# Tile 5's h and half of tile 7's normalised x: transposed by DMA instead of by TensorE

## The reference, cut to what matters

```
def fake_quant(x, s, z): q = clip(round(x / s + z), 0, 255); return (q - z) * s
x = x + tanh(g_xattn) * matmul(fake_quant(layernorm(x)), fake_quant(ctx))      # ctx: (2, 2048, 2048)
W = U * S[None, :] @ V.T                                                      # rank 512
x = x + tanh(g_ffn) * einsum('bti,oi->bto', layernorm(x), W)
```

## Time and profile before

| what | value |
|---|---|
| median of 3 runs | 588.23 us |
| the profiled execution's own time | 588.18 us |
| its span | 586.4 us |
| TensorE (PE) busy | 568.3 us, 97% |
| VectorE (DVE) busy | 447.8 us, 76% |
| ScalarE (ACT) busy | 236.0 us, 40% |
| GpSimd (POOL) busy | 196.3 us, 33% |
| chain that ended last | 94% PE, 2% DMA, 1% POOL |

### The profile page before, as it was taken

The page is one execution under the profiler, slowest core; times in us unless marked ns, Lnnn a source line. Parts: engine busy times, 40 slices in busy tenths (PEclk is TensorE's granted clock), DMA queues, the critical chain, the costliest instruction groups (busy, mean ns, idle before and its releaser), DMA issues.

```text
span 586.4 us, 7496 instructions
## 1 busy us (share of the span) xinstructions
PE 568.3 (97%) x2688; PEld 259.5 (44%) x2688; DVE 447.8 (76%) x797; ACT 236.0 (40%) x268; POOL 196.3 (33%) x146
## 2 busy tenths in 40 slices
PE   1899999999999999999999999999999999999998
PEld 0344444444444444444444444444444444444444
DVE  6959999997178982679978799798597986888222
ACT  4799888822123423648713612102530135103200
POOL 2989850000406127847541720220044005310000
PEclk9999999999999999999999999999999999999999
DMA  8999995638927796789975262423854086403722
GB/s 275 387 386 387 337 268 130 127 102 172 272 66 216 175 247 188 210 232 386 268 166 156 57 138 57 125 74 64 224 108 135 9 176 165 125 1 69 165 55 107
DMA packets 145941, 102.73 MB, mean 175 GB/s; under 512 B 108785, under 2 KB 109041, under 8 KB 145905
## 3 DMA queue, kind: packets, MB, share of 16 engines
q1 hardware_dynamic: 136912, 84.96, 55.0%
q10 hardware_dynamic: 8992, 17.30, 9.0%
HBM read 58.99 MB, written 16.78 MB: 129 GB/s over the span
## 4 chain that ended last, share of the span: by engine, by line
PE 94%; DMA 2%; POOL 1%; SPq 1%; issue 1%; DVE 0%; DVEq 0%
PE bank L616 23%; PE bank L692 19%; PE bank L661 12%; PE bank L697 9%; PE bank L755 9%; PE bank L760 9%; PE bank L756 9%; PE bank L579 2%; DMA v_hl<-in_ctx_dram 2%; SPq L331 1%; POOL u8r L270 1%; POOL q L279 1%; PE bank L711 0%; PE bank L592 0%; SPq L341 0%
## 5 line engine op out<-in xcount | busy, mean ns | idle before, releaser
L285 POOL TENSOR_SCALAR ring<-ring,bvec 128x2048 f32<-128x2048 f32 x16 | 33.4, 2089 | 259.2 <-DVE bvec L1245 259.2
L616 PE MATMUL bank<-q,qT 128*128 128x512 f16 x512 | 117.8, 381 | 0.0
L692 PE MATMUL bank<-v_hl,xT 128*128 128x512 f16 x448 | 101.3, 379 | 0.0
L290 POOL TENSOR_TENSOR ring<-ring,corr 128x512 f32<-128x512 f32 x64 | 88.9, 1419 | 22.6 <-ACT corr L967 21.6
L755 PE MATMUL bank<-u_hl,hbuf 128*128 128x512 f16 x208 | 78.9, 379 | 0.0
L756 PE MATMUL bank<-u_hl,hbuf 128*128 128x512 f16 x208 | 78.8, 379 | 0.0
L279 POOL TENSOR_SCALAR q<-u8r,const 128x1024 f16<-128x1024 uint8 x52 | 66.8, 1295 | 33.6 <-ACT u8r L864 29.8
L616 PEld LDWEIGHTS bank<-q,qT 128*128 128x128 f16 x512 | 50.3, 98 | 61.4 <-issue 1.7
L692 PEld LDWEIGHTS bank<-v_hl,xT 128*128 128x128 f16 x448 | 43.8, 98 | 52.2
L915 ACT ACTIVATE ln<-ln,const 128x1 f32<-128x1 f32 x16 | 4.7, 295 | 144.0 <-DVE ln L1342 144.0
L1416 DVE SCALAR_TENSOR_TENSOR ring<-bank,cy,ring 128x512 f32<-128x512 f32 x63 | 46.2, 745 | 17.4 <-PE bank L760 17.3
(11 more groups left out here) (173 smaller groups left out, 782.4 us busy)
## 6 DMA issues: line engine op xcount, KB each, us to landing
out_dram<-ring SPq DMA_DIRECT2D x63, 256.0 KB, 3.4
ring<-in_x_dram SPq DMA_DIRECT2D x62, 256.0 KB, 4.3
v_hl<-in_ctx_dram SPq DMA_DIRECT2D x26, 512.0 KB, 11.5
stage<-in_ctx_dram ACTq DMA_DIRECT2D x17, 512.0 KB, 5.9
u_hl<-in_L_ffn_V_dram SPq DMA_DIRECT2D x8, 512.0 KB, 11.4
corr<-in_ctx_dram ACTq DMA_DIRECT2D x8, 512.0 KB, 6.7
stage<-in_ctx_dram SPq DMA_DIRECT2D x6, 512.0 KB, 11.4
q<-in_ctx_dram ACTq DMA_DIRECT2D x4, 512.0 KB, 9.9
```

Source lines behind the costliest of these rows:

```text
L290: nc.gpsimd.tensor_tensor(xq(t, n), xq(t, n), corr[:, n * W:(n + 1) * W], ALU.add).then_inc(x1_pre, 1)
L616: mm = nc.tensor.matmul(unit_bank(t, n)[:, :], qT_of(t)[:, k, :], q2[:, n, k, :], start=(k == 0), stop=(k == KT - 1))
L692: nc.tensor.matmul(h_bank(u)[:, :], x_home(u, g)[:, half, k % 8, :], v_hl[:, k, 0, :], start=(g == 0 and a == 0 and half == 0), stop=False)
```

## The change

`H_PE`, `X_PE` and `h_pieces`, `hT_copy` are gone. Tile 5's h goes by DMA into its place in `qT` (that of the quantised row of tile 6), as soon as tile 6's stage 1 is done. Half 0 of tile 7's x goes by DMA into the place of tile 7's quantised row, once tile 7's stage 1 is done. Half 1 is still transposed by TensorE, in one call ahead of `mm4(5)`, and copied by VectorE into `xT`. All waits on counts are renumbered to fit. The diff, cut to its core:

```
-        AFTER = (TB + 1,) + tuple(second_of)
-        x_home = lambda u, g: xT[:, 0 if u in AFTER else g, :, :, :] if u not in AFTER or g else \
+        AFTER = (TB - 1, TB + 1) + tuple(second_of)
+        x_dma = lambda u, g: u + 1 - (g == 1 and u >= TB - 1)
+        x_home = lambda u, g: xT[:, 0 if u in AFTER and u > TB else g, :, :, :] if u not in AFTER or g else \
             qT_of(u).rearrange("p (a k) w -> p a k w", a=2)
...
-                elif u in h_home:
-                    sp.wait_ge(s1_done, S1_END(u))
+                elif u == TB - 3:
+                    sp.wait_ge(s1_done, S1_END(u + 1))
...
             x_transpose(6)
-            for n in range(NQ):
-                store(4, n)
-            for n in range(NQ):
-                load_x(8, n)
+            h_transpose(5)
+            store(4, 0)
+            store(4, 1)
+            x_transpose_half(7, 0)
+            store(4, 2)
+            store(4, 3)
+            load_x(8, 0)
...
-            h_pieces(5)
             mm3(6)
-            x_pieces(0)
+            x_pieces()
             mm4(5)
-            x_pieces(1)
             mm3(7)
...
-            hT_copy(5)
             x_hi_half(7, 1)
...
-            xT_copy(0)
+            xT_copy()
...
-            xT_copy(1)
             quantise(8)
```

More of the change, by code:

```diff
@@ L29, in gated_block_program @@
     NST = 10
-    H_PE = (5,)
-    X_PE = TB - 1
     NU8 = 8
@@ L124, in gated_block_program @@
         xT_in = [sem(f"xT_in{g}") for g in range(2)]
-        hT_in = sem("hT_in")
-        hT_written = sem("hT_written")
-        hT_copied = sem("hT_copied")
         xT_written = sem("xT_written")
         xT_copied = sem("xT_copied")
+        hT_in = sem("hT_in")
         y_stored = [[sem(f"y_stored{i}_{n}") for n in range(NQ)] for i in range(R)]
@@ L200, in gated_block_program @@
         h_bank = lambda u: bank[3 + u % 2]
-        x_dma = lambda u: u + 1 - (u > X_PE)
-        x_bank = lambda g, half: bank[(2 * g + half) % 3]
-        h_dma = lambda u: u + 1 - sum(v <= u for v in H_PE)
         y_bank = lambda i: bank[5 + i % 3]
@@ L367, in x_transpose_half @@
                     sp.wait_ge(mm3_half, 2 * (u - 1) + 1)
+                elif u - 1 in AFTER and u > TB:
+                    sp.wait_ge(mm3_half, 2 * u)
                 elif u >= 1:
@@ L493, in _ @@
             x_transpose(6)
-            for n in range(NQ):
-                store(4, n)
-            for n in range(NQ):
-                load_x(8, n)
+            h_transpose(5)
[5 more added lines that the diff above has]
+            load_x(8, 0)
+            load_x(8, 1)
+            load_x(8, 2)
+            load_x(8, 3)
             h_transpose(6)
@@ L586, in colsum_of_sums @@
                 if n < 2:
-                    pe.wait_ge(xT_copied, 4)
+                    pe.wait_ge(xT_copied, 2)
                 else:
@@ L678, in mm3 @@
                     pe.wait_ge(h_lo, u - 1)
-                if u - 2 in H_PE:
-                    pe.wait_ge(hT_copied, H_PE.index(u - 2) + 1)
                 if u == TB:
@@ L683, in mm3 @@
                 for g in range(2):
-                    if u == X_PE:
-                        pe.wait_ge(xT_copied, 2 * g + 2)
+                    if u == TB - 1 and g == 1:
+                        pe.wait_ge(xT_copied, 2)
                     else:
-                        pe.wait_ge(xT_in[g], 16 * x_dma(u))
+                        pe.wait_ge(xT_in[g], 16 * x_dma(u, g))
                     for a, k in enumerate(KORD[g]):
@@ L699, in mm3, with x_pieces @@
                     mm.then_inc(mm3_half, 1)
-            def x_pieces(g):
-                pe.wait_ge(xs_hi, 2 * X_PE + g + 1)
-                pe.wait_ge(xs_lo, 2 * X_PE + g + 1)
-                for half in range(2):
[L705 to L709, removed]
+            def x_pieces():
+                u = TB - 1
+                pe.wait_ge(xs_hi, 2 * u + 2)
+                pe.wait_ge(xs_lo, 2 * u + 2)
+                pe.wait_ge(x1_ready, S1_END(u))
+                for half in range(2):
+                    dst = bank[half][:, :].bitcast(f16)
                     for k in range(8):
-                        mm = nc.tensor.transpose(dst[:, k * P:(k + 1) * P], xs[:, g, half, k * P:(k + 1) * P], ident[:, :])
+                        mm = nc.tensor.transpose(dst[:, k * P:(k + 1) * P], xs[:, 1, half, k * P:(k + 1) * P], ident[:, :])
                     mm.then_inc(xT_written, 1)
[L714 to L722, removed]
             def mm4(u, n0=0, n1=NQ):
[L725 to L728, removed]
+                pe.wait_ge(hT_in, 16 * (u + 1))
                 for n in range(n0, n1):
@@ L926, in x_hi_half @@
                     act.wait_ge(p_done, 2 * NP * (first_of[u] + 1))
-                if u - 1 == X_PE:
-                    act.wait_ge(xT_written, 2 * g + 2)
+                if u == TB and g == 1:
+                    act.wait_ge(xT_written, 2)
                 elif u > 0:
-                    act.wait_ge(xT_in[g], 16 * x_dma(u - 1))
+                    act.wait_ge(xT_in[g], 16 * x_dma(u - 1, g))
                 nc.scalar.activation(xs[:, g, 0, :], xhalf(u, g), ACT.Identity, bias=bias, scale=scale).then_inc(xs_hi, 1)
@@ L941, in hid_hi @@
                 act.wait_ge(mm3_half, 2 * u + 2)
[L942 to L945, removed]
+                if u > 0:
+                    act.wait_ge(hT_in, 16 * u)
                 else:
@@ L949, in hid_hi @@
                     .then_inc(h_hi, 1)
[L951 to L955, removed]
             def column_correction(b, n):
@@ L1302, in t4 @@
                             for g in range(2):
-                                dve.wait_ge(xT_in[g], 16 * x_dma(PAIRS[p][0] - 1))
+                                dve.wait_ge(xT_in[g], 16 * x_dma(PAIRS[p][0] - 1, g))
                         else:
@@ L1376, in x_lo, with xT_copy @@
                 x_lo_half(u, 1)
-            def xT_copy(g):
+            def xT_copy():
                 for half in range(2):
[L1380 to L1383, removed]
+                    dve.wait_ge(xT_written, half + 1)
+                    dve.wait_ge(mm3_half, 2 * (TB - 2) + 2)
+                    nc.vector.tensor_copy(x_home(TB - 1, 1)[:, half, :, :].rearrange("p k w -> p (k w)"),
+                                          bank[half][:, :].bitcast(f16)).then_inc(xT_copied, 1)
             def hid_lo(u):
@@ L1396, in k_sum @@
                 elif i == 1:
-                    dve.wait_ge(xT_written, 2 + 2 * (n // 3))
+                    if n == 3:
+                        dve.wait_ge(xT_written, 2)
+                    else:
+                        dve.wait_ge(xT_in[0], 16 * TB)
                 else:
```

## The result

The changed kernel takes 592.68 us (median of 6 runs, 591.74 to 593.96) against 588.32 us (587.89 to 588.61) for the kernel before: a ratio of 1.0074, 95% interval 1.0064 to 1.0085. The forecast was 586.9 us. The 24 pieces are gone, and 4.4 us came in.

A forecast was written before the change was run, and what follows sets the result against it. TensorE, busy 568.3 of 586.4 us, was taken to bound the kernel. Own time 588.18 less 1.34 us of pieces gives 586.84; the median stands 0.05 above, so 586.9 us, all other terms nothing; range 586.4 to 588.3.

The forecast's parts named there:

- What TensorE loses, 1.34 us: TensorE's list drops 8 pieces of h (0.45 us) and 16 pieces of x (0.89 us), 1.34 us together.
- the whole gain reaches the end: After 341.26 us VectorE is pulled forward too, so all 1.34 us shorten the kernel's end.
- Tile 5's h: Its DMA fits SP's idle time, lands by 261.8 us, 9.6 us before mm4(5) wants it, and costs nothing.
- The slack of tile 7's transpose, 10.7 us: Half 0 of tile 7's x lands by 266.6 to 271.3 us, mm3(7) wants it at 281.97: no cost.
- The load on the DMA engines: Both transposes occupy the engines 4.2 us, 2.3 us fit before 260 us, so ScalarE's context loads slip 1.9 us (0 to 4.2).
- The place where a slip bites: TensorE would stall at mm4(6)'s fourth unit, through tile 6's y unit, only from a slip of 2.9 us.
- The slower rival: Loads and transposes hinder one another, slip passes 4.2 us; at 5.5 us TensorE waits 2.6 us: 589.5 us, chance 0.09.
- The rule of one set of 16 engines: DMAs of all issuers interleave on the same 16 engines, so the slip reaches ScalarE's loads despite their own queue.

The follow-up runs named there:

- the last version: Changed kernel with tile 7's transpose issued earlier, five ScalarE loads held until it landed, tile 6's upper half and tile 8's quantising ahead of chunks: 587.08 us, ratio 0.9976.
- the run with x alone: Changed kernel with tile 5's h back on TensorE and ScalarE, only half 0 of tile 7's x going by DMA: 592.26 us, ratio 1.0063.
- the extra transpose: Kernel before with all its TensorE pieces, plus one unused DMA transpose of half 0 of tile 7's x on SP: 591.36 us, ratio 1.0049.
- SP's order altered: Changed kernel with tile 7's transpose issued ahead of tile 4's stores on SP, ScalarE's loads not held: 591.02 us, ratio 1.0043.

## Why the prediction was wrong

- *What TensorE loses, 1.34 us:* right. In the last version mm3(7) starts at 282.02, 1.29 us ahead of the earlier trace rows, and 1.2 us reach the end, so "the whole gain reaches the end" held too.
- *Tile 5's h:* right. It went into SP's idle time at 254.20 and cost nothing.
- *The slack of tile 7's transpose, 10.7 us:* right in what it says, since TensorE never waited for that DMA. But the landing was put at 8.1 to 12.8 us at most and took 16.0.
- *The load on the DMA engines:* this is the step that failed. The prediction priced the transpose at 2.9 us of the engines, from a place where it runs alone, bounded the slip by 4.2 us, and took 1.9. Beside the loads it was an estimated 7.9 us. The slip of ScalarE's chunk at 283.59 was 10.1 us, or 9.4 without the later start. The trace of before had the row that says so, the 129 GB/s at a share of 1.25, and it was not read, because the share alone was. The 1.9 was also too small by the prediction's own prices: most of the 2.3 us of free time lies ahead of 258.5 us, when tile 7's transpose is issued, and from there to 260 us the share is 0.86, which leaves 0.2 us. That makes the slip 2.9 - 0.2 = 2.7 us, still under the 2.9 at which a wait was expected.
- *The place where a slip bites:* half right. The fourth unit of mm4(6) did wait, 0.58 us. But the first to wait was mm4(5)'s fourth unit, 23 us earlier, through tile 6's upper half on ScalarE, queued behind five chunks of the stream. The prediction followed only ScalarE's tail from 283.59 on. It gave ScalarE's issues no price, and so did not ask what else stood behind a blocked one. Where the issues were blocked less, the fourth unit of mm4(6) is the only place, as predicted: 2.96 us in the run with x alone.
- *The clock:* left out. In the profiled execution a wait of 3.49 us brought 1.7 us more. Of the changed kernel's six runs, four had a mean clock of 0.997, the other two 1.0. These two took 591.74 and 592.59 us, so most of the loss is there without the clock.
- *The slower rival* named the right mechanism, loads and transposes hindering one another beyond their own time, with a price of 2.6 us and a chance of 0.09. The price was too small and the chance far too low. The sentence against it, "the added work is only 4.2 us", used the number that was wrong.
- *The rule of one set of 16 engines* (Trainium skill, DMA: Bandwidth & Descriptors, "Issuing engines are not separate DMA queues") held: a transpose on SP's queue delayed ScalarE's. The word interleave in it was the warning, and the prediction took it as a sum of busy times.

What stays open is why a transposing packet takes three times as long beside loads, and a load's packet twice as long beside a transpose. The runs show that it does, that a copy does not, and that the outcome of the collision varies (landings of 9.9 to 16.0 us at nearly one place), not the cause. Whether loads from another place or fewer at once would do the same was not tried.

## What to carry to other kernels

Price a DMA from the rows where it runs beside what it will run beside, and read GB/s next to share. At a full share loads moved 386 and 405 GB/s here, a transpose alone 213 (the kernel before, 330.4 to 332.4 us), and the two together in the changed kernel 97 to 151: a rate under both is a sign of a collision. Moving work from the bounding engine to the DMA engines pays if it is put where they are idle, or if the transfers that it would meet are held until it has landed. On an engine that also issues DMAs, put what the bounding engine waits for ahead of the work that waits for a landing.

## What the runs showed of the hardware

A DMA transpose of 512 KB landed after 4.3 us alone, after 5.8 us with ScalarE's loads held, and after 9.9 to 16.0 us with ScalarE's 512 KB loads in flight; a plain copy of the same bytes beside them landed after 5.8. In the runs with a colliding transpose ScalarE's issue of four loads took 3.2 to 4.6 us instead of 2.5, and 4.7 beside the copy. A single load took up to 3.27 us to issue instead of 0.37. In this time ScalarE starts nothing else. TensorE's granted clock fell to its lower level after waits of 2.40, 2.96 and 3.49 us (the extra transpose, x alone, the changed kernel), but stayed at 1.00 after one of 2.71 us (SP's order altered) and after those of about 1 us. The lower level as the extra transpose's run shows it, after its wait of 2.40 us:

```profile
282.00:284.00 2.00, 1.82 (x7) 0.81 (x8) 1.90 (x3) 1.17 (x1) 0.93 (x1) 0.80 1.15 295
284.00:286.00 2.00, 2.00 (x6) 0.72 (x5) 2.00 (x4) 1.43 (x3) 1.65 (x2) 0.50 1.20 234
286.00:288.00 2.00, 2.00 (x21) 1.37 (x20) 1.93 (x7) 1.49 (x2) 1.37 (x2) 0.85 1.30 127
```
